# One transformer block on one core: the parts after the first attention in f16 with token-major results, ordered stage by stage

## The reference

```python
x = x + attn_a(layernorm(x))   # 16 heads of 64, causal, with biases and output weights Wo
x = x + ffn(layernorm(x))      # relu(x @ w1 + b1) @ w2 + b2, 128 -> 512 -> 128
x = x + attn_b(layernorm(x))   # one head: scores = (x @ W_qk) @ x.T / sqrt(128) + (kpos - qpos) * slope,
                               # causal softmax, values x @ W_v.T
x = x + ffn(layernorm(x))      # the same weights again
```

## Time and profile before

| | |
|---|---|
| median of 3 runs | 599.29 us (599.08 to 599.47) |
| the profiled execution, own time | 598.35 us |
| its span (first to last instruction) | 596.6 us |
| granted TensorE clock, mean | 0.973 |
| PE busy | 550.6 us (92%), 6314 matmuls |
| DVE busy | 468.8 us (79%) |
| ACT busy | 458.6 us (77%) |
| POOL busy | 400.9 us (67%) |
| HBM read and written | 12.21 and 9.44 MB |

### The profile page before, as it was taken

The page is one execution under the profiler, slowest core; times in us unless marked ns, Lnnn a source line. Parts: engine busy times, 40 slices in busy tenths (PEclk is TensorE's granted clock), DMA queues, the critical chain, the costliest instruction groups (busy, mean ns, idle before and its releaser), DMA issues.

```text
span 596.6 us, 16752 instructions
## 1 busy us (share of the span) xinstructions
PE 550.6 (92%) x6314; PEld 392.8 (66%) x6314; DVE 468.8 (79%) x1440; ACT 458.6 (77%) x877; POOL 400.9 (67%) x382
## 2 busy tenths in 40 slices
PE   4788999899999999999999999989799998789796
PEld 3454666566666766676667667656688776657674
DVE  4578888788888888888888888873378798688674
ACT  3668889889899989998998999889355883264485
POOL 5669899778888888888888888889500231066310
PEclk9989999999999999999999999999899997799799
DMA  8622323233342432333333424304571000000001
GB/s 194 159 54 66 88 82 106 55 90 91 91 107 59 113 98 74 106 92 90 91 84 92 112 55 116 88 31 169 194 240 44 1 1 0 1 1 1 2 19 53
DMA packets 35328, 47.89 MB, mean 80 GB/s; under 512 B 10776, under 2 KB 16688, under 8 KB 35248
## 3 DMA queue, kind: packets, MB, share of 16 engines
q1 hardware_dynamic: 33136, 46.29, 28.7%
q10 hardware_dynamic: 2112, 0.54, 0.5%
HBM read 12.21 MB, written 9.44 MB: 36 GB/s over the span
## 4 chain that ended last, share of the span: by engine, by line
PE 68%; DVE 12%; issue 9%; ACT 8%; POOL 2%; DMA 1%; SPq 0%; DVEq 0%; ACTq 0%; POOLq 0%
PE psum L531 9%; PE psum L587 8%; PE psum L588 8%; PE psum L485 7%; PE psum L487 6%; PE psum L486 6%; PE psum L569 5%; PE psum L567 5%; PE psum L568 5%; PE psum L743 2%; PE psum L590 2%; ACT p L1007 2%; DMA w_raw<-in_L_attn_a_Wk 1%; DVE st_lo L1144 1%; ACT p_hl L1008 1%
## 5 line engine op out<-in xcount | busy, mean ns | idle before, releaser
L1577 POOL TENSOR_TENSOR p_hl<-p,p_hl 128x512 f16<-128x512 f32 x288 | 326.2, 1158 | 46.9 <-ACT p_hl L1008 43.4
L1161 DVE CUSTOM_DVE_ANT_0 max_junk<-psum,mask_s 128x1024 bf16<-128x1024 f32 (+7 forms) x256 | 190.2, 753 | 32.6 <-issue 32.4
L1007 ACT ACTIVATE p<-psum 128x512 f32<-128x512 f32 x288 | 177.0, 615 | 17.1 <-PE psum L590 14.1
L1008 ACT ACTIVATE p_hl<-psum 128x512 f16<-128x512 f32 x288 | 178.1, 618 | 0.0
L567 PE MATMUL psum<-v_all,p_hl 128*128 128x65 f16 x1152 | 125.9, 194 | 2.8 <-POOL p_hl L1577 2.8
L568 PE MATMUL psum<-v_all,p_hl 128*128 128x64 f16 x1152 | 126.0, 193 | 0.0
L587 PE MATMUL psum<-q_hl,k_hh 128*128 128x512 f16 (+3 forms) x384 | 125.4, 327 | 0.5 <-ACT p_hl L1008 0.4
L569 PE MATMUL psum<-v_all,p_hl 128*128 128x65 f16 x1152 | 125.5, 195 | 0.0
L588 PE MATMUL psum<-q_hm,k_l 128*128 128x512 f16 (+3 forms) x384 | 122.1, 327 | 0.0
L567 PEld LDWEIGHTS psum<-v_all,p_hl 128*128 128x128 f16 x1152 | 107.9, 98 | 17.7 <-POOL p_hl L1577 3.0
L568 PEld LDWEIGHTS psum<-v_all,p_hl 128*128 128x128 f16 x1152 | 107.1, 98 | 4.8
(11 more groups left out here) (189 smaller groups left out, 1091.4 us busy)
## 6 DMA issues: line engine op xcount, KB each, us to landing
k_hh<-st_hi SPq DMA_DIRECT2D x64, 128.0 KB, 2.3
o_scratch<-o_sb SPq DMA_DIRECT2D x16, 512.0 KB, 2.6
o_in<-o_scratch SPq DMA_DIRECT2D x4, 2048.0 KB, 8.8
k_l<-st_lo SPq DMA_DIRECT2D x32, 128.0 KB, 2.4
q_hl<-st_hi SPq DMA_DIRECT2D x32, 128.0 KB, 2.3
q_hl<-st_lo SPq DMA_DIRECT2D x32, 128.0 KB, 2.4
q_hm<-st_hi SPq DMA_DIRECT2D x32, 128.0 KB, 2.4
x_sb<-in_L_attn_a_x SPq DMA_DIRECT2D x4, 256.0 KB, 3.8
```

The source lines that it names most:

```text
L1007: nc.scalar.activation(p32[:, ring_at(u, r), :], src, ACT.Exp, scale=SCALE_A).then_inc(exp_done, 1)
L1008: nc.scalar.activation(p_hl[:, u % 2, 0, BANK * r:BANK * (r + 1)], src, ACT.Exp, scale=SCALE_A).then_inc(phi_done, 1)
L1161: nc.vector.tensor_tensor_reduce(out=max_junk[:, n % 2, 0:cols], in0=max_banks(v, j, 0, cols), in1=mask_s[:, S - cols:S], scale=1.0, scala ...
L1577: nc.gpsimd.tensor_tensor(p_hl[:, u % 2, 1, cols], p32[:, ring_at(u, r), :], p_hl[:, u % 2, 0, cols], ALU.subtract)\
```

## The change

Everything behind the head loop is written anew, and a few lines in it.

- *Types.* wo, w1, w2, wqk, wv2, oT, xT, h, qb, qm_b and k_one are f16 where they were F32R. To keep f16 in its range the five weights are scaled by powers of two (`tail_gains`), found from sums of squares (`tail_squares` on ACT, in head 30, after two exponentials), a matmul with ones, and a power on POOL. Results are scaled back in the instructions that take them out of PSUM (`out_scale`, `score_scale`, and in outputs_out_b an added scaling of the denominator). xT2_hi/lo go; the tail uses xT_hi/lo again.
- *Weights.* w1 and w2 are no longer loaded at the start; Wo, w1 and w2 are loaded in head 29 and split (`tail_high` on ACT, `tail_low` on DVE) in head 31 and among the first steps behind it.
- *Token-major results.* In the output projection and both second products of the feed-forward, the activations are the stationary operand (128 tokens) and the weights the moving one (128 columns). One tile of 128 tokens is 24 products of 128 columns (output projection) or 12 (feed-forward). The result lies as x does: yT, turn_result and result_high go, and DVE adds half a chunk (two tiles) at a time from PSUM. The biases bo and b2 are added to x_sb by POOL as rows (`add_output_row`, `add_forward_row`).
- *Norms.* All 12 later norms are taken by ACT (`late_norm`, four instructions of 128 columns) from a shift that POOL makes (`chunk_shift`), and no longer by DVE.
- *Low halves.* h_lo of the second feed-forward is made by POOL, that of the first still by DVE. bias_s and bias_t are scaled by POOL.
- *Banks.* One bank (2) for all turned norms, one (7) for queries and values, two in place of three for scores and for the first product of the feed-forward. h_hi and h_lo have rings of eight, oT holds two whole chunks.
- *Order.* Each engine's order behind the head loop is a written list. In every stage the four chunks come in turn, and the results, norms and queries of the next stage follow (`K_ORDER`, `LN_ORDER`). Nine blocks of o_in are turned between the outputs of the last head; queries, values and the first maximum of attention b stand among the last steps of the first feed-forward, the first hidden blocks of the second feed-forward among the last outputs of attention b.
- *Loads.* o_in of chunks 0 and 1 is loaded in heads 28 and 29 (chunk 1 was loaded after the last head's scores). The result is stored in eight DMAs in place of four.

The diff, cut:

```diff
-    QB_BANKS, V2_BANKS, OB_BANKS = (0, 5), (1, 4), ((7, 1), (3, 5))
+    LB, QVB = 2, 7
+    TR_BANKS, H_BANKS, H_RING = (3, 4, 7), (5, 6), 8
+    Y_BANKS = ((0, 1), (0, 1), (0, 3))
+    S_BANKS, OB_BANKS = ((5, 6), (3, 4)), ((1, 0), (1, 7))
+    K_ORDER = tuple((stage, c) for stage in range(3) for c in range(CHUNKS))
+    k_of = {stage_chunk: n for n, stage_chunk in enumerate(K_ORDER)}
+    LN_ORDER = tuple((stage, c) for stage in range(4) for c in range(CHUNKS))
+    ln_of = {stage_chunk: n for n, stage_chunk in enumerate(LN_ORDER)}
...
-    BLOCKS = 3
-    BLOCK_BANKS = (0, 1, 4)
+    S_RING = 3
+    H32_RING = 3
...
-    wo_hi = sb("wo_hi", [P, OB, E], F32R)
+    wo_hi = sb("wo_hi", [P, OB, E], F16)
...
-                if u == HEADS - 2:
-                    sp.wait_ge(piece_lo, 4 * PAIRS)
+                if u == HEADS - 4:
                     for n in range(2):
                         sp.wait_ge(scratch_out[n], 16 * (PP // 2))
                     load_outputs(0)
+                if u == HEADS - 3:
+
+                    sp.wait_ge(piece_lo, 4 * PAIRS)
+                    sp.wait_ge(v_lo_done, VUNITS)
+                    for n in range(2):
+                        sp.wait_ge(k_moved[n], 48 * PAIRS)
+                        sp.wait_ge(q_moved[n], 48 * PAIRS)
+                    sp.dma_start(wo_raw[:, :, :], Wo.rearrange("(k p) e -> p k e", p=P)).then_inc(late_in, 16)
+                    sp.dma_start(w1_raw[:, :], w1).then_inc(late_in, 16)
+                    sp.dma_start(w2_raw[:, :, :], w2.rearrange("(m p) e -> p m e", p=P)).then_inc(late_in, 16)
+                    load_outputs(1)
-            load_outputs(1)
             store_pair(PAIRS - 1)
...
-            for u in range(HEADS):
-            for step in range(NU):
-                outputs(HEADS - 1, step)
...
+            pe.wait_ge(mrow_done, HEADS)
+            pe.wait_ge(tail_sq, 6)
+            nc.tensor.matmul(bank(MISC)[:, 0:6], ones[:, :], tail_sums[:, :], start=True, stop=True).then_inc(prep_full, 1)
+            pe.wait_ge(small_in, 80)
+            nc.tensor.transpose(bank(MISC)[:, P:2 * P], wv2_raw[:, :], ident[:, :]).then_inc(prep_full, 1)
+            pe.wait_ge(tail_made, 1)
+            nc.tensor.matmul(bank(MISC)[:, 2 * P:3 * P], ones[:, :], bo_diag[:, :], start=True, stop=True).then_inc(prep_full, 1)
+            pe_slot(HEADS - 1)
...
+                if n >= 3:
+                    pe.wait_ge(ot_lo_done, n - 2)
+                for j in range(CT):
+                    last = nc.tensor.transpose(bank(TR_BANKS[n % 3])[:, P * j:P * (j + 1)], o_in[c % 2][:, blk, j, :], ident[:, :])
+                last.then_inc(ot_full, 1)
...
+            def output_tile(c, j):
+
+                if j == 0:
+                    pe.wait_ge(ot_lo_done, OB * (c + 1))
+                    pe.wait_ge(wts_lo_done, 1)
+                result_free(k_of[0, c], j)
+                rows, cols = slice(P * j, P * (j + 1)), slice(P * (j % 2), P * (j % 2) + P)
+                for blk in range(OB):
+                    last = three(bank(Y_BANKS[0][j // 2])[:, cols], oT_hi[:, c % 2, blk, rows], oT_lo[:, c % 2, blk, rows], wo_hi[:, blk, :], wo_lo[:, blk, :],
+                                 start=(blk == 0), stop=(blk == OB - 1))
+                last.then_inc(y_full, 1)
...
+                pe.wait_ge(xn_ready, n + 1)
+                pe.wait_ge(xt_lo_done, n)
+                for j in range(CT):
+                    last = nc.tensor.transpose(bank(LB)[:, P * j:P * (j + 1)], xn[:, n % 2, j, :], ident[:, :])
+                last.then_inc(xt_full, 1)
...
+                if n >= 2:
+                    pe.wait_ge(h_hi_done, n - 1)
+                blk, cols = slice(P * m, P * (m + 1)), slice(BANK * c, BANK * (c + 1))
+                three(bank(H_BANKS[n % 2]), w1_hi[:, blk], w1_lo[:, blk], xT_hi[:, cols], xT_lo[:, cols]).then_inc(h_full, 1)
...
+                for m in range(FW):
+                    r = (FW * y + m) % H_RING
+                    last = three(bank(Y_BANKS[1 + y // CHUNKS][j // 2])[:, cols], h_hi[:, r, rows], h_lo[:, r, rows], w2_hi[:, m, :], w2_lo[:, m, :],
+                                 start=(m == 0), stop=(m == FW - 1))
+                last.then_inc(y_full, 1)
...
+                    pe.wait_ge(v2_lo_done, c)
+                three(bank(QVB), wqk_hi[:, :], wqk_lo[:, :], xT_hi[:, cols], xT_lo[:, cols]).then_inc(qb_full, 1)
...
-                        last = nc.tensor.transpose(bank(BLOCK_BANKS[n % BLOCKS])[:, P * j:P * (j + 1)], o_in[c % 2][:, blk, j, :], ident[:, :])
-                    three(bank(2 + c % 2), wo_hi[:, blk, :], wo_lo[:, blk, :], oT_hi[:, m, :], oT_lo[:, m, :],
-                          start=(blk == 0), stop=(blk == OB - 1)).then_inc(ot_used, 1)
-                    if blk == 3 and c >= 1:
-                        turn_result(c - 1)
...
+            turn_block(0, 0)
+            turn_block(0, 1)
+            turn_block(0, 2)
+            turn_block(0, 3)
+            outputs(HEADS - 1, 0)
...
+            turn_block(1, 0)
+            outputs(HEADS - 1, 6)
+            outputs(HEADS - 1, 7)
+            outputs(HEADS - 1, 8)
+            turn_block(1, 1)
+            turn_block(1, 2)
+            output_tile(0, 0)
+            turn_block(1, 3)
+            output_tile(0, 1)
+            turn_block(1, 4)
+            output_tile(0, 2)
+            turn_block(1, 5)
+            turn_block(1, 6)
+            turn_block(1, 7)
+            output_tile(0, 3)
+            output_tile(1, 0)
+            output_tile(1, 1)
+            output_tile(1, 2)
+            output_tile(1, 3)
+            turn_late(ln_of[1, 0])
+            turn_block(2, 0)
+            turn_block(2, 1)
+            turn_block(2, 2)
+            hidden(0, 0)
...
+            hidden(3, 0)
+            queries_b(0)
+            hidden(3, 1)
+            hidden(3, 2)
+            forward(2, 0)
+            forward(2, 1)
+            values_b(0)
+            forward(2, 2)
+            turn_late(ln_of[2, 1])
+            hidden(3, 3)
+            forward(2, 3)
+            queries_b(1)
+            forward(3, 0)
+            max_tile_b(0, 0)
+            forward(3, 1)
+            forward(3, 2)
+            forward(3, 3)
+            max_tile_b(0, 1)
+            values_b(1)
+            turn_late(ln_of[2, 2])
+            max_tile_b(0, 2)
...
+            turn_late(ln_of[3, 0])
+            outputs_b(1, 0)
+            outputs_b(1, 1)
+            hidden(4, 0)
+            hidden(4, 1)
+            outputs_b(1, 2)
+            outputs_b(1, 3)
+            hidden(4, 2)
+            outputs_b(1, 4)
+            hidden(4, 3)
...
+                for n, raw in enumerate((wo_raw, w1_raw, w2_raw, wqk_raw, wv2_raw, b1_sb)):
+                    nc.scalar.activation(junk, raw, ACT.Square, accum_out=tail_sums[:, n:n + 1]).then_inc(tail_sq, 1)
...
+                nc.scalar.mul(hi[:], raw[:], tail_gains[:, n:n + 1]).then_inc(wts_hi_done, 1)
+
+            for u in range(HEADS - 2):
                 act_slot(u)
-
-
-                nc.scalar.activation(yT[:, n % 2, :], bank(2 + n % 2), ACT.Identity, bias=bias, scale=scale).then_inc(yT_ready, 1)
+            exponentials(HEADS - 2, 0)
+            exponentials(HEADS - 2, 1)
+            tail_squares()
+            for r in range(2, NU):
+                exponentials(HEADS - 2, r)
...
+                nc.vector.scalar_tensor_tensor(out=x_sb[:, tiles, :], in0=bank(Y_BANKS[stage][half], 2 * P).rearrange("p (t e) -> p t e", e=E),
+                                               scalar=out_scale[:, n:n + 1], in1=x_sb[:, tiles, :], op0=ALU.mult, op1=ALU.add).then_inc(res_done, 1)
...
-                nc.vector.reciprocal(ob_den[:, m % 2:m % 2 + 1], src[:, E:V2W]).then_inc(ob_inverse, 1)
+                nc.vector.tensor_scalar(ob_den[:, m % 2:m % 2 + 1], src[:, E:V2W], tail_gains[:, 4:5], None, ALU.mult).then_inc(ob_scaled, 1)
+                dve.wait_ge(ob_scaled, m + 1)
+                nc.vector.reciprocal(ob_inv[:, m % 2:m % 2 + 1], ob_den[:, m % 2:m % 2 + 1]).then_inc(ob_inverse, 1)
-                nc.vector.scalar_tensor_tensor(out=ob_out[:, m % 2, :], in0=src[:, 0:E], scalar=ob_den[:, m % 2:m % 2 + 1],
-                                               in1=l1_cols[:, :], op0=ALU.mult, op1=ALU.mult).then_inc(ob_read, 1)
...
+            def late_rstd(n):
+                chunk_rstd(n)
+                chunk_shift(n)
...
+            def hidden_low(y, m):
+                nc.gpsimd.tensor_tensor(h_lo[:, n % H_RING, :], h32[:, n % H32_RING, :], h_hi[:, n % H_RING, :], ALU.subtract).then_inc(h_lo_done[y // CHUNKS], 1)
```

1294 lines of the change are left out of this document (845 added, 449 removed).

## The result

The changed kernel takes 579.9 us (median of 4 runs, 578.7 to 581.0) where the kernel before takes 599.2 (596.8 to 599.5): ratio 0.969, 95% interval 0.965 to 0.972. It is faster, as forecast, and 6.7 us slower than the 573.2 of the forecast.

The account below looks back on a forecast made before the run. PE was taken to bound the output projection and first feed-forward, DVE attention b, POOL the last stage: 426.6 + 58.7 + 5 = 490.3, then 543.3, then 570.5; with time around the span and run median, 573 us, range 557 to 592.

Parts of the forecast that it names:

- The rival built on dear products: Tail: narrow products cost 0.081 us each, 18 us more, 591; chance 0.17, shared with the case of too tight an order.
- The near-dense rival: Whole tail: order so good that losses vanish, 2 us in place of 5 before 490, DVE at 97%; 565 and below; 0.14.
- the stop-and-go rival: Tail: PE stops and goes, its clock falls to 1.2 of 2.4 GHz; slower than before, 608 with 35 us more; chance 0.05.
- The last two heads: End of head loop: squares add 2.5 us in head 30, nine blocks turned in head 31; outputs end 426.6, not 424.6.
- To the end of the first feed-forward: From the last head's outputs: PE bounds with 58.7 us of work plus 5 idle, ending at 490.3 against 493.7 before.
- sign of trouble: Output projection's loads: o_in landing after 443 would show the forecast wrong.
- Attention b: Attention b: DVE bounds it, 48.8 us of work at 92% busy, 53.0 us, ending at 543.3.
- The second feed-forward: Last stage: POOL bounds it with 26 us of work; starts at 534.8, ends at 570.5; stage does not shrink.
- POOL the busiest engine: Sign of being right: POOL the busiest engine in the last 30 us.
- Two more signs of being right: Last head's outputs end 1 to 4 us later; DVE busy for 88% or more until about 543.
- The order couples too tightly: Attention b and last stage: few banks let late engines stop others, 60.8 and 39.1 us, median 593; 0.17 with dear products.

Follow-up runs that it names:

- gains_late: Six of the seven small DVE instructions of tail_gain moved behind the last head's outputs, against the changed kernel: 575.8 us, ratio 0.965.
- den_ones: Changed kernel with attention b's denominator scaled by the product itself, through the ones column of the values, without DVE's separate scalings: 579.0 us, ratio 0.968.
- q_late: Changed kernel with queries and values of chunks 2 and 3 moved behind attention b's first scores: 583.6 us, ratio 0.976.
- low1_pool: Changed kernel with eight low halves of the first feed-forward (chunks 2 and 3) moved from DVE to POOL: 578.2 us, ratio 0.967.
- again: The changed kernel measured once more, with nothing altered, beside its variants: 579.0 us, ratio 0.970.
- diag_start: Changed kernel with tail_diagonal, one DVE instruction, moved ahead of the head loop: 581.3 us, ratio 0.971.
- low2_dve: Changed kernel with the 16 low halves of the second feed-forward moved from POOL back to DVE: 577.1 us, ratio 0.965.

## Why the prediction was right or wrong

*The sign, and the tail.* Narrow products start 0.056 us apart in the output projection, from 440.72 to 446.03 without a break (96 of them); 0.057 was taken from the earlier trace rows. The rule of the Trainium skill ("TensorE: Matmul & The Clock Gate", "Back-to-back issue gap": about 81 ns) does not hold for them. The rival built on dear products fell with that. Its own 0.081 was no half way either: worked out from the row, half clock would make 0.114 of 0.057, half way is 0.086, and the price some 22 us and not 18.

```profile
440.89 0.22 PE L509 MATMUL psum<-wo_hi,oT_hi 128*128 128x128 f16 x1
440.95 0.22 PE L510 MATMUL psum<-wo_hi,oT_lo 128*128 128x128 f16 x1
441.00 0.22 PE L511 MATMUL psum<-wo_lo,oT_hi 128*128 128x128 f16 x1
```

PE is busy for 60.4 us in the stretch for which 58.7 were summed, and idles 5.4 where 5 were allowed. The near-dense rival allowed 2. The clock is 1.00, 0.94 and 0.99 over the three parts of the tail, where the kernel before has 0.87 and 0.94 from attention b on; the stop-and-go rival did not come true. It was not empty, though: nearly all that the 0.94 lacks lies in the time before the first scores, where PE is busy for 10.4 of 15.3 us.

```profile
497.30:512.60 15.30, 10.40 (x56) 5.31 (x55) 12.26 (x33) 6.65 (x14) 1.70 (x4) 0.81 0.01 1
```

*The step that failed: "The last two heads".* 424.6 was to become 426.6 and became 431.5, and the profiled loop even stood 1.0 us earlier. Head 30: the prediction charged 2.5 us to squares on ACT and none to the rest, and the total is 2.95; that the two are near is luck. The squares do take what was summed on ACT (3.8 us, 399.38 to 403.18, for 3.9), but only 1.7 of it reaches head 31, the low end of the range given. The step named PE's preparatory products and said that head 31 would wait for ACT anyway; they were in fact in line, with a wait ahead of them (1.3). It did not name tail_diagonal, a lone DVE instruction ahead of the maxima, which costs nothing beside the squares and 1.1 us without them. Head 31: 14.9 us from the first exponential to the end of the outputs was to become 14.4 and became 19.8. With the loop 1.0 us early, 5.4 and 0.45 make the 4.9 of the table. The sum counted ACT and PE, and put DVE's small scalings into a sentence apart from it ("could each wait for a subtraction of POOL, some 8 us on a DVE that has 5 us free"). That is the term that was left out. They took 5.5 us, and gains_late gets 3.1 back. The rule quoted there (the Trainium skill, "SBUF — State Buffer", "SBUF: two separate sides") agrees with five of the seven: 1.07 to 1.20 us beside POOL, and the same in 0.14 to 0.22 without. The other two took 0.20 and 0.14 beside POOL too, so "each" was too much. The remaining 2.3 of the 5.4 were not taken apart; in gains_late PE still waits 1.45 us for the first low half and 0.59 for POOL.

*To the end of the first feed-forward.* 2.1 us over: 1.7 of it more PE work than summed, 0.4 more idling. The loads were a false sign. o_in for chunk 2 is issued at 436.65 and takes 8.1 us (8.8 in the earlier trace rows), so it lands near 444.8, later than the 443 named as a sign of trouble. PE asks for it at 446.7 and does not wait: everything had moved. The load of chunk 3 beside it takes 12.6 us and keeps nobody waiting either.

*Attention b.* 54.6 against 53.0. DVE's work was 47.0 us (48.8 summed) at 86%, not 92%. That DVE bounds the stage fails behind the first biased unit, as den_ones shows, and is untested ahead of it: in those 15.3 us DVE is busy for 12.3, PE for 10.4 at a clock of 0.81, and q_late, which took work out of them, won 1.1 at a clock of 0.66. The sum by one engine's list came near the length, with two errors against each other, and gave the wrong price for an edit. The 12 us that the first scores were to wait are 13.4 on PE (497.3 to 510.6).

*The second feed-forward.* 26.9 against 27.2, and the low halves on POOL hold it, with 1.7 us to the next. The sign "POOL the busiest engine" is a draw: 20.06 us against PE's 20.08. Two more signs of being right failed: the last head's outputs ended 6.9 us later and not 1 to 4, and DVE was busy for 86% of attention b and not 88% or more.

*The rivals.* "The order couples too tightly" was priced in the wrong place (attention b, the last stage). It did happen, at the hand-off, where one late engine held two others.

## What to carry to other kernels

In an order written by hand, price every instruction that stands ahead of a hand-off, on every engine, also the one-column ones: beside a busy POOL a DVE instruction on SBUF can cost a whole POOL instruction (five of seven did here), and what others wait for goes ahead of it. Two delays that lie side by side look free or nearly so when one of them is taken away; take both away before calling either harmless, and don't add up what each gave alone. A stage's length may follow from the list of one engine although an edit of that list changes little, since the next engine is close behind; only taking work away tells.

## What the runs showed of the hardware that was not expected

- Whether POOL stretches a DVE instruction can change from run to run: of the ten profiled runs that have the seven small scalings beside POOL's subtractions, the sixth took 1.19 us in eight and 0.14 in two (den_ones, low1_pool), with the same lists up to there. The outputs of the last head end at 32.9 and 33.3 in those two, and at 34.0 to 34.4 in the five others of that kind (changed, again, diag_start, low2_dve, q_late). The fourth and the seventh, which read one column of SBUF, took 0.20 and 0.14 in all ten runs; whether their form or their place behind a stretched one spares them was not tested.

```profile
419.40 0.14 DVE L1666 TENSOR_TENSOR out_scale<-tail_inv 128x1 f32<-128x1 f32 x1
```

- A scaling of 1024 columns by a column of scalars takes POOL 2.86 and 3.80 us, 2.5 and 3.3 times a 512-column subtraction (1.16). DVE did the same in 0.75 each in the kernel before.

```profile
446.25 2.86 POOL L2074 TENSOR_SCALAR bias_s<-bias_s,slope_g 128x1024 f32<-128x1024 f32 x1
```

- The same wait of 2.2 us on PE in head 30 was followed by a clock of 1.00 in one profiled run and of 0.58 over the next 4 us in another.
